# Two moves in the first attention stage: a VectorE reduction goes ahead of a row of PSUM copies, and the load of the next batch goes behind one more group of stores

## The reference

```python
q, k, v = (proj(Wq), proj(Wk), proj(Wv))
content = jnp.einsum('bhld,bhmd->bhlm', q, k)
rel_k = jnp.einsum('bhld,lmd->bhlm', q, a_k)
rel_q = jnp.einsum('bhmd,lmd->bhlm', k, a_q)
pos_pos = jnp.einsum('lmd,lmd->lm', a_q, a_k)
logits = (content + rel_k + rel_q + pos_pos) * scale
attn = jax.nn.softmax(logits, axis=-1)
out = jnp.einsum('bhlm,bhmd->bhld', attn, v) + jnp.einsum('bhlm,lmd->bhld', attn, a_v)
```

## Time and profile before

| what | value |
|---|---|
| median of 3 runs | 5536.31 us (5531.79 to 5537.22) |
| the profiled execution: its time, its span | 5536.31 us, 5534.4 us |
| PE busy | 5010.9 us, 91% |
| DVE busy | 4013.9 us, 73% |
| POOL busy | 3415.9 us, 62% |
| ACT busy | 3023.3 us, 55% |
| mean granted TensorE clock | 0.957 of full speed |

### The profile page before, as it was taken

One profiled execution on the slowest core, in us unless ns is written; L12 is line 12 of the kernel. 1 busy time (PEld: TensorE's weight loads), 2 busy tenths in 40 slices (PEclk: granted clock), 3 DMA queues, 4 the chain that ended last, 5 costly groups with the idle time before them and its releaser, 6 DMA issues. The chain is left out here.

```text
span 5534.4 us, 210241 instructions
## 1 busy us (share of the span) xinstructions
PE 5010.9 (91%) x86640; PEld 4190.3 (76%) x86640; DVE 4013.9 (73%) x7792; ACT 3023.3 (55%) x5561; POOL 3415.9 (62%) x2140
## 2 busy tenths in 40 slices
PE   5999999976999999999999999999999995888858
PEld 3888888865888888888888888888888884555536
DVE  3777777766888888888888888888888885544543
ACT  1333333324666666666666666666666663656631
POOL 1111111118899999998999999989999993212200
PEclk9999999988999999999999999999999997888967
DMA  1000000003222322232222222222222220000000
GB/s 41 6 6 6 6 6 6 6 19 88 63 62 62 79 67 62 62 79 66 63 62 72 72 62 62 73 70 62 63 69 64 63 61 17 1 0 0 0 5 15
DMA packets 365187, 241.36 MB, mean 44 GB/s; under 512 B 147206, under 2 KB 360852, under 8 KB 363932
## 3 DMA queue, kind: packets, MB, share of 16 engines
q1 hardware_dynamic: 362348, 232.89, 17.2%
q10 hardware_dynamic: 2480, 3.02, 0.2%
HBM read 24.56 MB, written 4.21 MB: 5 GB/s over the span
## 5 line engine op out<-in xcount | busy, mean ns | idle before, releaser
L1192 POOL TENSOR_TENSOR b_rnorm<-b_ss,neghalf 128x16 f32<-128x16 f32 x384 | 1118.5, 2913 | 75.7 <-DVE b_ss L1686 64.7
L1188 POOL TENSOR_TENSOR b_rot<-b_t 128x1024 f32<-128x1024 f32 x384 | 907.6, 2364 | 139.6 <-DVE b_t L1675 134.3
L1673 DVE TENSOR_TENSOR b_t<-psum,b_cosg 128x1024 f32<-128x1024 f32 x384 | 470.4, 1225 | 451.0 <-ACT b_sq L1553 448.1
L1197 POOL TENSOR_TENSOR b_qk<-b_rot,b_rnorm 128x1024 f32<-128x1024 f32 x384 | 731.8, 1906 | 57.9 <-POOL b_rnorm L1192 6.4
L1553 ACT ACTIVATE b_sq<-psum 128x1024 f32<-128x1024 f32 x384 | 394.0, 1026 | 511.7 <-PE psum L1308 511.5
L1303 PE MATMUL psum<-b_w_hi,b_xT_parts 128*128 128x512 f32 x1152 | 524.3, 455 | 30.9 <-issue 22.6
L365 POOL TENSOR_TENSOR a_k_diag<-a_k_parts,a_head_rows 128x1024 fp32r<-128x1024 f32 x64 | 119.9, 1896 | 676.4 <-PE psum L502 605.0
L1680 DVE TENSOR_REDUCE b_ss<-b_sq 128x16 f32<-128x1024 f32 x384 | 464.3, 1209 | 0.0
L1308 PE MATMUL psum<-b_w_hi,b_xT_parts 128*128 128x512 f32 x1152 | 459.3, 399 | 2.4 <-issue 2.4
L1304 PE MATMUL psum<-b_w_lo,b_xT_parts 128*128 128x512 f32 x1152 | 457.1, 397 | 2.0 <-issue 2.0
L1387 PE MATMUL psum<-b_wo,b_oT 128*128 128x128 f32 x3072 | 425.3, 281 | 0.8 <-ACT b_oT L1571 0.8
(11 more groups left out here) (235 smaller groups left out, 12354.0 us busy)
## 6 DMA issues: line engine op xcount, KB each, us to landing
b_v_win<-b_v SPq DMA_DIRECT2D x2304, 65.0 KB, 2.0
b_v_win<-b_v SPq DMA_DIRECT2D x1152, 32.5 KB, 1.8
oa<-XR SPq DMA_DIRECT2D x1024, 2.0 KB
xcur<-X SPq DMA_DIRECT2D x112, 128.0 KB, 2.0
b_wqkv<-in_L_ffn_Wqkv_dram SPq DMA_DIRECT2D x6, 1536.0 KB, 6.4
b_wo<-in_L_ffn_Wo_dram SPq DMA_DIRECT2D x12, 256.0 KB, 2.9
out_dram<-X SPq DMA_DIRECT2D x4, 512.0 KB, 3.2
b_w<-in_L_ffn_W_dram SPq DMA_DIRECT2D x6, 341.0 KB
```

Source lines behind the costliest of these rows:

```text
L1188: nc.gpsimd.tensor_tensor(rot[:, i, :, :], t1[:, i, :, :], t2[:, i, :, :], ALU.add).then_inc(rot_done, 1)
L1192: nc.gpsimd.tensor_tensor(rnorm[:, i, :], ss[:, i, :], neghalf[:, :], ALU.pow).then_inc(rn_done, 1)
L1197: nc.gpsimd.tensor_tensor(qk[:, i, :, :], rot[:, i, :, :], rnorm[:, i, :, None].broadcast_to((P, 16, BD)), ALU.mult).then_inc(qk_done, 1)
L1673: nc.vector.tensor_tensor(t14, x4, tab(cosg, slice(0, BD), BD), ALU.mult)
```

## The change

Two moves, no instruction added or removed. On DVE `sums(0)`, the reduction of group 0, goes from behind `maxima(2)` to behind `relative_keys(1)`, ahead of `blocks(qb)` and `maxima(2)`. On SP `next_x(b + 2)` goes from between `stores(b, 1)` and `stores(b, 2)` to between `stores(b, 2)` and `stores(b, 3)`.

```diff
                         maxima(1, b)
                         outputs(0)
                         relative_keys(1)
+                        sums(0)
                         if ahead:
                             blocks(qb, q_blk)
                         maxima(2, b)
-                        sums(0)
                         outputs(1)
                         if ahead:
                             blocks(kb[:2], k_blk)
@@
                     with sp.Fori(0, B - 2) as b:
-                        stores(b, 0)
-                        stores(b, 1)
+                        for g in range(3):
+                            stores(b, g)
                         next_x(b + 2)
-                        stores(b, 2)
                         stores(b, 3)
```

## The result

The changed kernel takes 5613.31 us (median of 4 runs, 5606.26 to 5617.28) against 5534.05 us (5530.22 to 5537.22): a ratio of 1.0135, 95% interval 1.0114 to 1.0154. It is slower, as forecast, but by 79 us and not by 49; the time lies above the range of 5566 to 5602. The ratio is an estimate over the executions; it can differ by up to 0.1% from the ratio of the medians, which is 1.0143 here. Three more executions are on record: the profiled one of 5614.55 us, whose span is 5612.6 us, one of 5607.92 and one of 5591.35. The last of these, alone of the seven, lies inside the range.

What follows compares the result with a forecast made beforehand. The prediction took PE, busy 91% of the span and nearly without a hole in the loop, as the bound. It added 24.8 us (DVE move) and 24.5 us (SP move), 49.3 us, to 5536.31 us: 5585.6 us, range 5566 to 5602.

Steps and rivals of the forecast that it cites:

- the clock: PE's granted clock behind the new waits, about 1.7 and 2.04 us: no fall expected, nothing added to the sum.
- both new waits of PE: PE's waits for the query blocks, about 1.7 us, and for x, 2.04 us, some 45 us apart.
- the stalls for x: PE's first transpose of x waits for the later load: 12 stalls of 2.04 us, +24.5 us.
- The third rival: The clock falls at each of 12 stalls for x: 19 to 30 us more, 5605 to 5616 us; 6%.
- The rule of the Trainium skill: After a DMA wait in each loop pass, every pass starts at the low clock: 1.6 to 2.5 us more per stall.
- What a late query block costs PE: DVE's query blocks come 1.75 us later and PE loses it; 1.65 us net per loop sequence, 15 times, +24.8 us.
- What frees a bank sooner: Group 1's mask multiply on DVE runs sooner; PE's second transposes gain 0.10 us, not 0.8, as ACT becomes the next wait.
- At the back edges: At b = 5 and b = 10 PE is held 3.48 and 3.62 us anyway; x arrives beneath that, no added stall.
- The other rivals: Only DVE move costs, 5561 us, 5%; only SP move, 5561, 3%; faster, 5524, 3%; nothing measurable, 5536, 3%.

Runs made afterwards that it cites:

- e6_pe_unrolled: The kernel before with the three passes of PE's loop written out, so without a back edge: 5524.45 us, ratio 0.9969.
- e8_dve_filled: The kernel before with the DVE move alone and 14 unread transposes on PE at the wait for the query blocks: 5559.29 us, ratio 1.0027.
- e1_dve_only: The changed kernel without the move on SP, so the DVE move alone: 5571.92 us, ratio 1.0065 to the kernel before.

## Why the prediction was wrong

**The step that failed is the clock.** It said that "both new waits of PE [...] are shorter than the one without a fall, so I add nothing". It rested on one wait of 2.76 us without a fall. One row could not carry that: the same wait stands in all ten profiles and brings the clock down in two, `e6_pe_unrolled` and `e8_dve_filled`, while the stalls for x do in 10 of 12, and 7 of these 10 are shorter than 2.76 us. Waits of 1.4 us bring it too, at times. The third rival had both the mechanism and the price, 1.6 to 2.5 us at each stall and 5605 to 5616 us in all; I gave it 6%. That the measured 5613 lies in it is in part luck: the falls brought some 16 us and not 19 to 30, longer stalls and the code behind the stage the rest. The rule of the Trainium skill that I set aside there ("TensorE: Matmul & The Clock Gate", section "HAM oscillation — how this bites in real kernels") describes this case better than the row that I held against it, though the waits of its example are longer, some 3 to 5 us, and not each pass starts low here: 10 of 12. Filling the waits shows it, since more work takes less time: 1.0077 with both filled against 1.0135 and 1.0109 in the two measurements of the changed kernel.

The profiled execution is 78.2 us over before, 28.9 more than the forecast's 49.3: 16.2 from falls with the small rests, 7.0 behind the stage, 4.4 from longer stalls, 0.9 at the back edges, 0.4 from the DVE move. Without the 16.2 it would have taken 5598 us, inside the range.

**What a late query block costs PE was right.** Forecast 1.65 us with the small gain taken off, measured 1.68 (70.81 - 69.13). The two waits of 1.41 and 0.18 us carry it. My 1.74 in the expectations counted with it 0.06 us that come with the stall.

**What frees a bank sooner gives next to nothing, right.** 0.10 us was forecast, 0.08 measured. PE's wait for ACT takes the place of its wait for the mask multiply.

**The stalls for x were right in place, count and cause, and too small in size.** 2.04 us was forecast, and 1.98 to 2.06 us measured where SP issues 16 stores in 7.70 us. In 6 of 12 batches the issues take 8.3 to 8.7 us, since one or more of them are slow, and the stall is 2.62 to 3.00 us. Together 28.9 and not 24.5 us. In the kernel before, the issues of group 2 take 8.3 to 8.8 us too in 6 of the 14 batches, all behind 520 us, and I had read the spacing in one batch near 380 us. What slows an issue stays open; in `e6_pe_unrolled` 13 of 14 groups take 7.73 us, so it is not in SP's code alone.

**At the back edges** the load hides beneath PE's own gap, nearly as forecast, at 0.9 us more for the two. These two loads are slower than the others, 3.6 and 3.9 us from issue to landing, and not the 2.10 that I took.

The other rivals fall with the counts: neither term is missing, and no kernel with either move has a median under before's.

What stays open is when a wait brings the clock down. In the changed kernel the stalls do and the shorter waits never; once the stalls are filled, the shorter waits do, 5 of 15. Length alone doesn't decide (2.00 us passed at 258.74 us, 1.39 us did not at 277.28 in `e1_dve_only`), and I have no run that sets where a wait comes and holds its length.

## What to carry to other kernels

Where TensorE works without a hole, price a new wait as its length plus the chance of a fall of the clock, here up to 1.71 us each, behind 4 to 10 of 12 waits of 2 to 3 us; one wait without a fall in the trace says little, so count many or take the price into the range. Before moving a load behind other issues on a queue, count the time of the issues themselves over several passes, slow passes too, and set the landing against the moment its reader wants it. A hardware loop's back edge on the bounding engine can be worth more than the order of the work within.

## What the runs showed that I had not expected

A fall of the clock has one price: each loss within the loop is 1.70 or 1.71 us, or twice that, whatever the wait before it was, 1.4 or 3.8 us. In time it costs that or a little less: a batch with a fall is 1.6 us longer in `e1_dve_only` and 1.7 in the changed kernel. Idle work on TensorE can make a kernel faster (20 and 14 transposes that nobody reads, 1.0135 to 1.0102 to 1.0077). And 16 store issues cost 7.7 us in a loop and 5.5 us written out, for the same stores.
